# Dealing out the output-projection products of a graph block, and making its quantiser scales ahead of a stage border

## The reference

```python
xn = layernorm(x)
# graph attention: scores of 4 heads for every edge, a softmax over the edges of one target node,
# then a weighted sum over them
e = einsum('ehd,hd->eh', leaky_relu(xl[src] + xr[dst]), att)
p = exp(e - segment_max(e, dst)[dst]); alpha = p / segment_sum(p, dst)[dst]
gnn = segment_sum(alpha * xl[src], dst) @ W_up
# linear attention of 16 heads
kv = einsum('shd,she->hde', phi(k), v); mix = einsum('shd,hde->she', phi(q), kv) @ Wo + bo
x = x + gnn + mix
# feed-forward with weights and activations rounded to 4-bit values, with one scale for 16 elements
x = x + nvfp4_ffn(layernorm(x), gate_w, up_w, down_w, s_in, s_in_down)
```

## Time and profile before

| | |
|---|---|
| median of 3 runs | 1055.31 us (1052.18 to 1057.67) |
| profiled execution: time, span | 1057.76 us, 1056.0 us |
| granted TensorE clock, mean | 0.971 |
| busy: PE, DVE, ACT, POOL | 962.3, 824.8, 648.7, 486.2 us |
| `maxima` | from 577.6 to 612.1 us of the span |
| `aggregate` | from 612.1 us on, to about 818 us |

### The profile page before, as it was taken

The page is one execution under the profiler, slowest core; times in us unless marked ns, Lnnn a source line. Parts: engine busy times, 40 slices in busy tenths (PEclk is TensorE's granted clock), DMA queues, the critical chain, the costliest instruction groups (busy, mean ns, idle before and its releaser), DMA issues. The chain is left out here.

```text
span 1056.0 us, 17499 instructions
## 1 busy us (share of the span) xinstructions
PE 962.3 (91%) x5429; PEld 795.7 (75%) x5429; DVE 824.8 (78%) x1395; ACT 648.7 (61%) x1435; POOL 486.2 (46%) x582
## 2 busy tenths in 40 slices
PE   2689779999999999999997879999999979999996
PEld 2576779999999999999997357888889434455443
DVE  5875567888887878888888777998985758887776
ACT  3264456666675766666665468999999235554442
POOL 0211677777777777777771624443344100110000
PEclk9999889999999999999998789999999999999999
DMA  9403587989889898989973669989986254674314
GB/s 238 65 8 105 162 255 242 282 272 270 274 261 278 276 281 271 293 285 276 285 246 103 257 177 329 297 279 304 289 284 206 77 135 118 148 164 116 81 19 79
DMA packets 109977, 221.40 MB, mean 210 GB/s; under 512 B 25883, under 2 KB 58228, under 8 KB 109857
## 3 DMA queue, kind: packets, MB, share of 16 engines
q1 hardware_dynamic: 89053, 159.98, 47.2%
q0 software_dynamic: 20576, 60.08, 23.7%
q10 hardware_dynamic: 260, 0.20, 0.1%
HBM read 156.56 MB, written 62.95 MB: 208 GB/s over the span
## 5 line engine op out<-in xcount | busy, mean ns | idle before, releaser
L1024 POOL DMA_INDIRECT score_gath<-xl_rows,misc x324 | 347.7, 1073 | 101.6 <-issue 95.1
L1064 PE MATMUL score_ps_m<-x_hi,score_w_hi 128*128 128x416 f32 (+1 forms) x576 | 209.5, 364 | 2.1 <-DVE score_w_lo L1217 1.9
L1066 PE MATMUL score_ps_m<-x_hi,score_w_lo 128*128 128x416 f32 (+1 forms) x576 | 204.5, 355 | 0.0
L1065 PE MATMUL score_ps_m<-x_lo,score_w_hi 128*128 128x416 f32 (+1 forms) x576 | 204.3, 355 | 0.0
L1800 ACT ACTIVATE agg_gath<-agg_gath,prob 128x64 f32<-128x64 f32 x648 | 159.4, 356 | 5.6 <-DMA agg_gath<-edge_rows 5.1
L1196 DVE TENSOR_TENSOR score_zb<-score_gath,score_ps_x 128x1024 f32<-128x1024 f32 x81 | 98.8, 1219 | 69.2 <-PE score_ps_x L1047 59.3
L1749 PE MATMUL ps_all<-agg_gath,agg_hot 128*125 128x128 f32 x648 | 128.3, 280 | 7.9 <-DVE agg_hot L1855 6.2
L1751 PE MATMUL ps_all<-agg_gath,agg_hot 128*125 128x136 f32 x648 | 129.6, 282 | 0.0
L1749 PEld LDWEIGHTS ps_all<-agg_gath,agg_hot 128*125 128x125 f32 x648 | 101.0, 190 | 24.1 <-issue 23.0
L1064 PEld LDWEIGHTS score_ps_m<-x_hi,score_w_hi 128*128 128x128 f32 x576 | 109.7, 190 | 4.5 <-issue 2.9
L2100 PE MATMUL ps_all<-mix_w,phi_c 128*125 128x512 f32 x240 | 108.1, 601 | 5.2 <-DVEq L2374 4.7
(11 more groups left out here) (341 smaller groups left out, 1653.9 us busy)
## 6 DMA issues: line engine op xcount, KB each, us to landing
edge_rows<-score_gath SPq DMA_DIRECT2D x81, 528.0 KB, 3.8
agg_gath<-edge_rows SPq DMA_DIRECT2D x81, 528.0 KB, 6.1
local_bc<-local_rows SPq DMA_DIRECT2D x40, 224.0 KB
score_gath<-xl_rows,misc POOLq DMA_INDIRECT x324, 4.6
phi_c<-phi_rows SPq DMA_DIRECT2D x10, 500.0 KB, 5.0
x_bo<-in_x SPq DMA_DIRECT2D x10, 500.0 KB
x_bo<-in_L_mix_bo POOLq DMA_DIRECT2D x10, 500.0 KB, 6.8
out<-fin_x SPq DMA_DIRECT2D x9, 500.0 KB
```

The lines of the kernel that those rows point to most:

```text
L1024: nc.gpsimd.indirect_dma_start(out=gath[:, g % GS, q, :], out_offset=None, in_=xl_rows, in_offset=bass.IndirectOffsetOnAxis(ap=src_idx[:, ...
L1064: pe.matmul(acc, w_hi[:, i % 2, kk, :], x_hi[:, kk, cols], start=(kk == 0), stop=False)
L1065: pe.matmul(acc, w_hi[:, i % 2, kk, :], x_lo[:, kk, cols], start=False, stop=False)
L1066: mm = pe.matmul(acc, w_lo[:, i % 2, kk, :], x_hi[:, kk, cols], start=False, stop=(kk == KC - 1))
```

## The change

The runs of products become 4, 3, 2 and 7 instead of 7, 2, 3 and 4. The five small operations that turn the three weight maxima into scale values move from the start of `aggregate` to `maxima`, between VectorE's last correction of the maxima and its differences. The block scales of the first weight matrix move from VectorE's work for group 0 to the end of `maxima`, behind the run maxima. For this the tile `small`, which holds the block scales, moves into the free last part of the score tensor, and a temporary tile `p2` is added. The values are the same.

```diff
--- before.py
+++ after.py
@@ -189,6 +189,7 @@
     k.w_scale = sb("w_scale", [P, 4, 3])
     k.bias_qkv = sb("bias_qkv", [P, 3, KC])
     k.part_iota = sb("part_iota", [P, 1])
+    k.w_small = k.score[:, :, :].rearrange("p i h -> p (i h)")[:, 1024:1024 + 2 * NJ * WB].rearrange("p (a b) -> p a b", a=2)
     k.w_tile = k.score[:, :, :].rearrange("p (a i) h -> p a (i h)", a=3)
     return k
 
@@ -1274,7 +1275,7 @@
 
         W = HEADS * TE
         R = PB * P
-        NM, FILL = 2 * PANELS, (7, 9, 12)
+        NM, FILL = 2 * PANELS, (4, 7, 9)
         WO = 4
         wo_dram = a["L0_mix_Wo"].rearrange("(k p) o -> k p o", p=P)
         wo = sb("wo", [P, WO, D])
@@ -1292,6 +1293,7 @@
         last_t = sb("last_t", [P, PB, TE])
         last = sb("last", [P, R])
         w_row = sb("w_row", [3, P])
+        p2 = sb("p2", [P, NJ * WB], BF16)
         w_col = sb("w_col", [3, 1])
         diff = fwd[:, :].rearrange("p (n h) -> p n h", h=HEADS)
         carried = pen_b
@@ -1516,6 +1518,12 @@
                 done.append(from_before(2))
                 from_behind(1, done[1])
                 from_behind(2, done[2])
+                v.wait_ge(s_wdone, 1)
+                q.do(v.reciprocal(k.w_scale[:, 3, :], k.w_scale[:, 0, :]))
+                q.do(v.tensor_scalar(k.w_scale[:, 1, :], k.w_scale[:, 3, :], 2688.0, None, ALU.mult))
+                q.do(v.tensor_scalar(k.w_scale[:, 2, :], k.w_scale[:, 1, :], 1.0 + 2.0 ** -22, None, ALU.mult))
+                q.mark(v.reciprocal(k.w_scale[:, 3, :], k.w_scale[:, 1, :]))
+                q.do(v.tensor_scalar(k.w_scale[:, 1, :], k.w_scale[:, 1, :], 1.0 / 6.0, None, ALU.mult))
                 for b in range(PB):
                     v.wait_ge(s_m_t, b + 1)
                     m = ps_a[:, b, :].rearrange("p (h i) -> p i h", h=HEADS)
@@ -1530,6 +1538,7 @@
                     q.mark(v.tensor_tensor(k.run_max[:, pairs, :], m,
                                            last[:, pairs].unsqueeze(2).to_broadcast([P, P, HEADS]), ALU.mult))
                 q.wait()
+                PairQuantiser(v, q, k.w_amax, k.w_small, None, p2[:, :]).scales(0, k.w_scale[:, 1, 0:1])
 
 
 NEAR_ONE = 1.0 + 2.0 ** -7
@@ -1626,7 +1635,7 @@
         work = sb("work", [P, 1024])
         coarse = sb("coarse", [P, 1024], BF16)
         xq = sb("xq", [P, 2, 1024], BF16)
-        small = sb("small", [P, 2, NJ * WB])
+        small = k.w_small
         zeros, node_iota = k.zeros, k.node_iota
         w_pair = [k.score[:, :, :].rearrange("p i h -> p (i h)")[:, 0:1024], k.misc[:, :]]
 
@@ -1836,11 +1845,6 @@
             @block.vector
             def _(v):
                 own = Steps(v, s_v)
-                own.do(v.reciprocal(k.w_scale[:, 3, :], k.w_scale[:, 0, :]))
-                own.do(v.tensor_scalar(k.w_scale[:, 1, :], k.w_scale[:, 3, :], 2688.0, None, ALU.mult))
-                own.do(v.tensor_scalar(k.w_scale[:, 2, :], k.w_scale[:, 1, :], 1.0 + 2.0 ** -22, None, ALU.mult))
-                own.mark(v.reciprocal(k.w_scale[:, 3, :], k.w_scale[:, 1, :]))
-                own.do(v.tensor_scalar(k.w_scale[:, 1, :], k.w_scale[:, 1, :], 1.0 / 6.0, None, ALU.mult))
                 quant = PairQuantiser(v, own, k.w_amax, small, work[:, :], coarse[:, :])
 
                 def weigh(g):
@@ -1860,9 +1864,7 @@
                     weigh(g)
                     one_hot(g)
                     m, kind, j = (g - 1) // 6, (g - 1) // 24, (g - 1) // 6 % 4
-                    if g == 0:
-                        quant.scales(0, k.w_scale[:, 1, 0:1])
-                    elif m < NP:
+                    if g and m < NP:
                         if g % 6 == 1:
                             v.wait_ge(s_wt[m % 2], 16 * (m // 2 + 1))
                             quant.scaled(w_pair[m % 2], k.w_scale[:, 2, kind:kind + 1], j)
```

## The result

The change made the kernel **0.36% slower**: 1058.74 us as the median of 9 runs (1056.69 to 1061.82) against 1054.57 us (1052.18 to 1059.84, 9 runs); ratio 1.0036, 95% interval 1.0021 to 1.0051, which is 2.2 to 5.4 us. The profiled execution shows little of that (span 1055.9 us, time 1057.66), since the profiled execution of before had itself been 3.2 us above its kernel's median (1057.76). So what follows compares stages, and more profiles of both kernels.

A forecast was written before the change was run, and what follows sets the result against it. The border was taken as set by the chain of the maxima, losing time twice behind products. Border -1.1 and group 7 +0.3 gave -0.8 us: 1054.5 us against the median of 1055.31, range 1051.2 to 1058.1.

The forecast's parts named there:

- The border comes 1.1 us sooner: End of the maxima stage, where every engine stops: last eviction forecast at 610.71 us against 611.85.
- The clock was in my rivals: Rival 2's claim that products 11 to 15, behind the exponential, run at the low clock, each 0.9 to 1.07 us more.
- 0.3 late: Behind the border: TensorE's start of group 7 taken as 0.3 us late, the middle of the forecast span.
- x's loads would swallow the savings of VectorE: Behind the border: x's loads bind groups 4 and 7, leaving at most 0.4 us if group 7's landing stays.
- TensorE's idle time ahead of group 4: Behind the border: TensorE, early, idles some 5 us, then loses 1.5 to 3 us at half clock.
- issuing it sooner moves it only forward in a line that does not move: Group 7's load queues behind x's on the DMA engines; issuing it sooner gains 0, landing stays 25.8 us behind the border.
- 0.4 early to 1.0 late: Behind the border: forecast span, in us, for TensorE's start of group 7.
- a fixed line: DMA behind the border: x's 125 rows sit on five engines, later loads queue there, so sooner issue gains 0.
- Rival 1: Behind the border: VectorE's saved work does count, -1.1 - 2.0 = -3.1 us, 1052.2 us; chance 0.17.
- Rival 2: Products behind the exponential run at the low clock: border 1.75 us later, +2.8 in all, 1058.1 us; chance 0.20.
- Rival 3: Scale values' 0.92 us and one slow product take the 1.1; stretch ends where it did, 1055.3 us; chance 0.18.

The follow-up runs named there:

- e1: The kernel before with only the products dealt out as 4, 3, 2 and 7, scales left behind the border; ratio 1.0018 to before.
- e6: The kernel after, with GpSimd's last round of index arithmetic held until VectorE has corrected the maxima; ratio 1.0010 to before.
- e2: The kernel after with the old deal of products (7, 2, 3, 4), scale values and block scales still ahead of the border; ratio 1.0041 to before.
- e9: The kernel after, with ScalarE evicting products 9 and 10 ahead of the exponential instead of behind it; ratio 1.0034 to before.
- e13: The kernel before with 16 idle products on TensorE at the end of the score stage's queue; ratio 0.9999 to before.
- e3: The kernel after, with group 6's edge load and all behind it held until x's second load has landed; ratio 1.0027 to before.
- e4: The kernel after with each early load of x issued as 112 and 13 rows instead of 125; 1051.58 us, ratio 0.9961 to before.
- e7: The kernel before with each early load of x issued as 112 and 13 rows instead of 125; ratio 0.9978 to before.
- e12: The kernel after, unchanged, run again for its profile alone; border at 34.6 us of the stage.
- e5: The kernel before, unchanged, run again for a second profile and its time; ratio 1.0000 to before.
- e11: The kernel before, unchanged, run again for its profile alone; border at 30.9 us of the stage.

## Why the prediction was wrong

It said 1054.5 us, 0.8 under the median it knew. Measured: 1058.74, and 0.36% above before. The order of events was as forecast, and so were many sizes; two steps failed, the base and size of the gain ahead of the border, and the landing of loads behind it.

- **"The border comes 1.1 us sooner" failed, in two ways.** First, the base. The 34.5 us of the old deal was the long form of that stretch. Over the five profiles it takes 32.5 us on average (34.5, 34.5, 30.9, 30.8, 32.0), over the three of after 34.6: **2.0 us more, not 1.1 less**. e1, with the deal alone, agrees: 34.4 us, and a loss of 1.9 us by its ratio (0.0 to 3.8). In the short form, products 4 to 6 hold the conditions for 1.00 to 2.00 us and not for 2.74 of the 3.59, because VectorE's own edge penalties end that shortly before, and product 11 holds nothing. So the new deal gives the chain next to nothing there: the exponential starts at 25.6 to 26.9 with the old deal in its short form and at 25.9 in e1. The five scale values (0.9 us) come on top: 26.5 with both. And from its start to the last eviction's end it is 4.85 us with two products left and 7.7 with five, both at full clock. I had worked out that payment, and set it against a gain that only the long form has to give. The clock was in my rivals, but at the new kernel's end and not in the old kernel's base.
- Second, in the long form itself (before and after both with the clock low until about 11): **the corrections did not just move, they grew by 1.0 us.** Starting 2.5 us sooner they ran beside GpSimd's arithmetic. e6 shows it by taking that away: 2.19 for 3.25. (In the short form of before they took 3.1 to 3.25 as well, so there the change adds nothing.) I had costed VectorE's work at its old durations and never asked what GpSimd was doing at the new place. In this pair the border stands at 34.5 in both: the forecast 1.1 less this 1.0, and 0.2 in small pieces.
- **Behind the border, "0.3 late".** That x's loads would swallow the savings of VectorE was right, and so was TensorE's idle time ahead of group 4 (7.54 us) and the low clock behind it. But "issuing it sooner moves it only forward in a line that does not move" is refuted: x's second load lands at 14.7 us when the loads behind it are held back. In before it lands at 17.5 on average, in after at 19.1. That the change's sooner issue makes this difference is likely but not shown: e2, e6 and e9 issue group 7's load at 7.5 to 7.7 us behind the border for 6.1 to 7.7 in after and 9.7 to 11.5 in before, and have x's at 17.6 to 18.1. Group 7's load lands 27.8 us behind the border on average, for 26.5, and TensorE starts group 7 at 29.8 for 27.4 in the first pair, 29.5 for 28.1 on average: 2.4 and 1.4 us late, where I gave 0.4 early to 1.0 late. By the end of the stage less is left: `aggregate` takes 206.8 for 206.2 us over the profiles, 0.6, within the 2.1 by which those of before differ.

The two stages together, 2.0 + 0.6 = 2.6 us, lie inside the interval of 2.2 to 5.4. They are means over five and three executions, and those of before differ by up to 3.7 us at the border. The missing 1.2 of the 3.8 is not accounted for. It does not lie in the other stages of these profiles: ahead of `maxima` and behind `aggregate` those of after are 0.6 and 0.9 us shorter, so that in all they are 1.2 us longer than those of before (1057.2 for 1056.0 on average). Nor is it known how many of the executions without a profile take the short form. What decides which form an execution takes stays open too: e13 shifted the low stretch and did not remove it.

The Trainium skill (DMA: Bandwidth & Descriptors, on why a DMA increments its semaphore by 16) gives 5 engines for 125 rows. This case agrees: in e3, with nothing behind x's loads, the DMA share is 0.31 to 0.32 from 618 to 622 us, about 5 of 16, and with the split of e4 and e7 the second load ends its wait at 12.0 to 12.2 us for 16.6 to 19.5. But the consequence I drew from it, a fixed line, was mine and wrong.

Rival 1, that VectorE's work does count, was the one that the experiments turned to account: it counts as soon as x's loads are out of the way (205.7 us without it, 201.4 with it). Rival 2 named low-clock products behind the exponential. They did not occur: in after and in e12 the five took 4.85 us at the full clock. The slow product of e9 stood ahead of the exponential. Rival 3, that the stretch ends where it did, is what the first pair of profiles shows, but its base was the long form too.

## What to carry to other kernels

Before costing a change of a few microseconds, look at more than one execution of the stretch: a stage whose pace hangs on the matrix engine's clock can have two lengths, and one profile shows one of them. When an instruction moves, ask what the other engines do at its new place, since its duration is not its own. And where work is hoisted across a border to feed a stage sooner, first clear what starts at the border itself: the hoist cost 0.4% alone (e2), and together with x's loads spread over more engines it gave 0.4% (0.8% with all the mends).

## What was not expected of the hardware

Eight VectorE operations on 128x128 f32 took 3.25 us beside GpSimd's arithmetic on a 1x324 tile, and 2.19 us with GpSimd idle. Few of them grew, but by much: 346 ns in the median and 949 at most, for 344 and 350. A 500 KB load of 125 rows landed up to 4.8 us later when more loads were issued behind it on the same queue (14.7 against 19.5 us); as 112 and 13 rows it had landed at 10.1 to 12.2 us in five kernels. TensorE's clock fell from 2.4 to 1.2 GHz (granted 1.0 and 0.50) in the same code at different places from one execution to the next: in the kernel before it was low from 0.2 to 10.4 us of the stage in e5, and from ahead of it until 4.4 in e11.
